# Where the last step of two layer norms runs: VectorE's subtract-and-multiply, or ScalarE's scale and bias per token

## The reference

```
def _layernorm(x, axis=-1, eps=1e-05):
    m = jnp.mean(x, axis=axis, keepdims=True)
    v = jnp.var(x, axis=axis, keepdims=True)
    return (x - m) / jnp.sqrt(v + eps)
...
x = _layernorm(x + _L0_attn_ref(x, W1, b1, Wp, bp))
x = _layernorm(x + _L0_ffn_ref(x, W_r, W_k, W_v, mu_r, mu_k))
```

## Time and profile before

| what | us |
|---|---|
| median of 3 runs | 761.15 |
| lowest and highest | 760.0, 762.69 |
| the profiled execution, its own time | 761.43 |
| its span in the profile | 759.7 |
| PE busy | 614.4 (81%) |
| DVE busy | 585.8 (77%) |
| ACT busy | 471.4 (62%) |
| POOL busy | 378.0 (50%) |

### The profile page before, as it was taken

How to read it: one execution, slowest core, us unless ns; L and a number is a source line. 1 busy time by engine, 2 the same in 40 slices (tenths; PEclk the granted TensorE clock), 3 DMA queues, 4 the chain that set the end, 5 groups by cost and what they waited for, 6 DMA issues and landing times.

```text
span 759.7 us, 17094 instructions
## 1 busy us (share of the span) xinstructions
PE 614.4 (81%) x6349; PEld 297.4 (39%) x6349; DVE 585.8 (77%) x1515; ACT 471.4 (62%) x918; POOL 378.0 (50%) x520
## 2 busy tenths in 40 slices
PE   2256888898888989898989888888989897987743
PEld 1013343444443535353434434443535353533232
DVE  3067888879889898979798989889898989792231
ACT  1110677686867676767777676767676776677510
POOL 6110334364555555565555464655655565455533
PEclk9999999999999999999999999999999999999755
DMA  2241213131322323131413131322323231100100
GB/s 55 92 101 44 91 54 115 44 113 45 98 73 60 112 58 115 51 121 36 120 33 118 41 128 45 79 93 58 113 58 115 45 109 33 47 17 16 29 14 14
DMA packets 63320, 53.29 MB, mean 70 GB/s; under 512 B 8706, under 2 KB 59012, under 8 KB 63236
## 3 DMA queue, kind: packets, MB, share of 16 engines
q1 hardware_dynamic: 63236, 52.20, 24.1%
HBM read 34.87 MB, written 17.30 MB: 69 GB/s over the span
## 4 chain that ended last, share of the span: by engine, by line
PE 50%; DVE 33%; ACT 6%; issue 5%; POOL 2%; DMA 2%; SPq 1%; POOLq 0%; DVEq 0%; ACTq 0%
DVE rowmax L632 16%; PE ops L481 12%; PE tps L433 8%; PE spare L372 8%; PE sps L450 8%; PE spare L386 5%; ACT probs L562 4%; DVE h L689 4%; DVE rowmax L636 3%; PE spare L412 2%; PE sps L457 2%; DVE result L689 2%; DVE attn L670 2%; DVE stats L643 2%; PE sps L462 2%
## 5 line engine op out<-in xcount | busy, mean ns | idle before, releaser
L562 ACT ACTIVATE probs<-tps 128x512 f32<-128x512 f32 x640 | 346.5, 595 | 139.4 <-PE tps L433 138.7
L632 DVE TENSOR_REDUCE rowmax<-sps 128x1 f32<-128x512 f32 (+2 forms) x768 | 342.5, 503 | 65.9 <-PE sps L462 62.2
L736 POOL TENSOR_SCALAR_AFFINE_SELECT probs<-probs 128x512 f32<-128x512 f32 x256 | 158.0, 635 | 262.6 <-ACT probs L562 262.6
L450 PE MATMUL sps<-kop,qop 48*128 48x128 bf16 (+3 forms) x1024 | 128.7, 310 | 62.5 <-DVE rowmax L632 35.7
L481 PE MATMUL ops<-probs,vop 128*32 128x384 f32 (+3 forms) x2048 | 172.7, 444 | 4.4 <-POOL probs L736 2.5
L433 PE MATMUL tps<-qop,kop 50*128 50x384 bf16 (+3 forms) x1024 | 126.4, 304 | 29.8 <-ACT probs L562 29.8
L636 DVE TENSOR_REDUCE rowmax<-sps 128x2 f32<-128x512 f32 x128 | 82.3, 685 | 15.6 <-PE sps L462 14.7
L433 PEld LDWEIGHTS tps<-qop,kop 50*128 50x128 bf16 x1024 | 34.5, 94 | 144.3 <-ACT probs L562 110.3
L450 PEld LDWEIGHTS sps<-kop,qop 48*128 48x128 bf16 x1024 | 40.5, 95 | 117.4 <-DVE rowmax L632 69.4
L457 PE MATMUL sps<-qmask,rows_of 64*128 64x256 bf16 (+1 forms) x640 | 83.7, 258 | 0.0
L481 PEld LDWEIGHTS ops<-probs,vop 128*32 128x32 f32 x2048 | 50.5, 109 | 77.4 <-issue 62.0
(11 more groups left out here) (73 smaller groups left out, 656.1 us busy)
## 6 DMA issues: line engine op xcount, KB each, us to landing
d_parts<-qk_parts SPq DMA_DIRECT2D x16, 768.0 KB, 3.5
qop<-d_parts SPq DMA_DIRECT2D x192, 32.0 KB
qop<-d_parts SPq DMA_DIRECT2D x64, 96.0 KB
kop<-d_parts SPq DMA_DIRECT2D x192, 32.0 KB
kop<-d_parts SPq DMA_DIRECT2D x64, 96.0 KB
xa<-L_attn_x SPq DMA_DIRECT2D x16, 256.0 KB, 3.0
xres<-L_attn_x SPq DMA_DIRECT2D x16, 256.0 KB, 3.4
out<-result SPq DMA_DIRECT2D x16, 256.0 KB, 2.5
```

The costliest lines, as they stand in the source:

```text
L450: nc.tensor.matmul(sps[:, bank(n + hh), off:off + w], qop[r, par, pair, BLK * a:BLK * a + BLK], kop[r, par, pair, 0:w], start=j == 0, stop ...
L562: nc.scalar.activation(probs[:, g % 2, i, :], tps[:, bank(4 * GROUPS * n + 4 * g + i), :], ACT.Exp, scale=SCALE)\
L632: last = nc.vector.reduce_max(rowmax[:, par, QUARTET * half + t, hh, a:a + 1], sps[:, bank(n), off:off + w], axis=AX_X)
L736: last = nc.gpsimd.affine_select(out=v, in_=v, compare_op=ALU.is_ge, fill=0.0, base=0, pattern=[[0, QUARTET], [1, BLK]], channel_multiplie ...
```

## The change

The form `(src - mean) * rstd`, one VectorE instruction for each 128 tokens, is replaced by `src * rstd + shift` on ScalarE, with `shift = -mean * rstd` formed on VectorE for the four blocks of 128 tokens in one instruction. `scale` and `bias` are given as one number per partition (token). The first norm keeps its place in group 7 but runs on ScalarE after the group's four exponentials; the second is in group 9 after its exponentials and ahead of `scale_steps`. VectorE's `shift` for the second norm is in group 8.

```
+            def normalise(i, n, src, dst, done_shift, done):
+                wait(act, done_shift, n + 1)
+                for t in range(TT):
+                    last = nc.scalar.activation(dst[:, t, :], src[:, t, :], ACT.Identity,
+                                                bias=shift[:, i, t:t + 1], scale=rstd[:, i, t:t + 1])
+                last.then_inc(done, 1)
...
+                    if g == 7 and active("D", b):
+                        wait(act, z_done, before("E", b))
+                        normalise(0, before("D", b), y, h[:, 1 - par], shift_done, h_done)
+                    if g == 9 and active("E", b):
+                        wait(act, stored, 16 * before("E", b))
+                        normalise(1, before("E", b), z, result, shift2_done, result_done)
                     if g == 9 and active("D", b):
                         scale_steps(before("D", b))
...
-            def normalise(i, n, src, dst, done_rstd, done):
+            def shift_of_mean(i, n, done_rstd, done_shift):
                 wait(dve, done_rstd, n + 1)
-                for t in range(TT):
-                    last = nc.vector.tensor_scalar(dst[:, t, :], src[:, t, :], moments[:, i, t, 0:1],
-                                                   rstd[:, i, t:t + 1], ALU.subtract, ALU.mult)
-                last.then_inc(done, 1)
+                nc.vector.scalar_tensor_tensor(shift[:, i, :], moments[:, i, :, 0], -1.0, rstd[:, i, :],
+                                               ALU.mult, ALU.mult).then_inc(done_shift, 1)
...
                     if g == 7 and active("D", b):
-                        wait(dve, z_done, before("E", b))
-                        normalise(0, before("D", b), y, h[:, 1 - par], rstd_done, h_done)
-                    if g == 9 and active("E", b):
-                        n = before("E", b)
-                        wait(dve, stored, 16 * n)
-                        normalise(1, n, z, result, rstd2_done, result_done)
+                        shift_of_mean(0, before("D", b), rstd_done, shift_done)
+                    if g == 8 and active("E", b):
+                        shift_of_mean(1, before("E", b), rstd2_done, shift2_done)
```

More of the change, by code:

```diff
@@ L180, in block_program @@
         rstd = sb("rstd", [P, 2, TT])
+        shift = sb("shift", [P, 2, TT])
         h = sb("h", [P, 2, TT, E])
@@ L235, in block_program @@
         rstd_done = sem("rstd_done")
+        shift_done = sem("shift_done")
         h_done = sem("h_done")
@@ L245, in block_program @@
         rstd2_done = sem("rstd2_done")
+        shift2_done = sem("shift2_done")
         result_done = sem("result_done")
```

## The result

| | us |
|---|---|
| changed kernel, median of 6 runs | 770.33 (767.13 to 774.01) |
| kernel before, beside it, 6 runs | 762.74 (760.0 to 764.36) |
| ratio, 95% interval | 1.0112 (1.0078 to 1.0146) |
| the profiled execution of the changed kernel | 767.13, span 765.4 |

The account below looks back on a forecast made before the run. TensorE and VectorE were the two busy engines (81% and 77%), with both norms on the chain. Terms summed to +3.75 us on the profiled 761.43, giving 765.2; 765.0 was predicted, range 757 to 774.

Parts of the forecast that it names:

- The price of the new instruction: On ScalarE: 495 ns for each 128x128 activation with two pointers, 0.385 us in a row, 1.54 us a norm.
- Rivals 1 and 2: ScalarE's small instructions: 1, cheap enough, not slower, 747 at the lower bound, chance 0.3; 2, no overlap, 778, chance 0.05.
- `shift`: On VectorE: 0.1 us for each, bounded by 0 and 0.16, with no wait to speak of.
- Group 8: In a full step, TensorE no longer waits 1.24 us for VectorE's maximum before `sps`; gain 0.74 us.
- Group 0: `result` ahead of `scaled` delays exponentials; TensorE waits some 1.6 us for ScalarE, leaving a full step at +0.02 us.
- The draining steps: End of b = 14 +0.8; b = 15 +0.1 and +0.95; b = 16 +0.7 and +0.4; last `result` +0.7 us.
- the sum: All terms over the whole kernel, full steps and those with fewer stages: 3.75 us slower, also given as 3.8.
- Rival 3: Group 8's gain is real and group 0 absorbs the delay: 0.1 to 0.2 us a step kept, 762 to 764; chance 0.15.
- Two of the signs named: Per full step: ScalarE busy +4.0 us, VectorE busy about -3.0; chain shares of both move by about 3 us each step.

Follow-up runs that it names:

- changed, again: The changed kernel, unedited, timed again on another occasion: 770.38 us, ratio 1.0106.
- changed, wait filled: Also called the filled kernel: the changed kernel plus 12 unused TensorE transposes in group 0 of b = 2 to 15; 766.50 us, ratio 1.0056.
- draining steps on VectorE: The changed kernel, but with `h` of b = 15 and 16 and `result` of b = 14 to 17 back on VectorE; 763.10 us, ratio 1.0028.
- `result` alone: The changed kernel with `h` back on VectorE, only `result` on ScalarE in group 9; 783.12 us, ratio 1.0262.
- one half: The changed kernel with `result` back on VectorE, only `h` on ScalarE; 752.77 us, ratio 0.9883.

## Why the prediction was right, and where its size was off

The profiles, cut at the start of `y` in b = 2 and in b = 14, say where the time went (us):

| profile | up to b = 2 | b = 2 to 14 | b = 14 to the end | span |
|---|---|---|---|---|
| before | 174.8 | 488.5 | 96.5 | 759.7 |
| changed | 173.7 | 488.8 | 102.9 | 765.4 |
| changed, again | 174.2 | 493.2 | 103.0 | 770.4 |
| changed, wait filled | 176.0 | 487.3 | 99.3 | 762.6 |

- **The price of the new instruction.** 495 ns alone and 1.54 us of ScalarE for a norm had been taken from the rows of other shapes; 487 ns and 1.54 us came out. Rivals 1 and 2, both about this price, fall with it. By the Trainium skill, "ScalarE: Activation LUTs", section "What ACT_TABLE_LOAD costs", the estimate is 479 ns, and 386 ns in a row; the trace agrees (487, and 1.54 / 4 = 385).
- **`shift`** took 155 ns, 0.05 more than taken, and nobody waited for it in a full step.
- **Group 8.** 0.74 us of gain forecast. TensorE's `osum` transposes start 5.18 us after group 7's exponentials (389.88 - 384.70), before 6.00 (391.92 - 385.92): 0.82.
- **Group 0.** The delay of the exponentials ate it up as forecast: the net of a full step is -0.10 us (+0.02 forecast), and from b = 2 to 14 the filled kernel, which has no fall there, needs 1.1 us less than the kernel before. The length of TensorE's wait was mis-stated as 1.6 us; it is 2.18. The prediction's own rows give it: the wait of 0.74 us ahead of `sps` goes away as well as the 0.74 of group 8, so TensorE comes to the place at 397.99 - 0.74 - 0.74 = 396.51, and the forecast start at 398.70 makes the wait 2.19. For the schedule this changes nothing, as ScalarE alone decides when the wait ends. For the clock it does.
- **The draining steps.** 3.6 us forecast (3.75 less the full steps and b = 1). From `y` of b = 14 to the end, the filled kernel needs 2.8 us more than the kernel before, but not at the same clock: in the kernel before, the clock fell at 704.6 us and for good at 714.8, in the filled one only at 719.3. The kernel with these norms back on VectorE held its clock there until 717.6. Against it the filled one needs 5.0 us more (99.25 and 94.24), where the same terms, with the 0.74 of group 8 that stays, had given 4.4. The changed kernel, with its falls, needs 6.4 more than before.
- **What failed is a term that is not in the sum: the clock.** It was priced at zero, with full steps taken as running at 1.00. The filled kernel is 3.9 us faster than the changed one by the medians, and what is left over the kernel before, 766.50 - 762.06 = 4.4, is near the 3.8 of the sum. So about half of the 8.3 us between the changed kernel and the kernel before goes with the idle time that the transposes fill. By the table it is lost in two places. In the full steps it is 1.5 us with one fall and 5.9 with three, one of them longer; from b = 14 on it is 3.6 and 3.7, and there the wait of 2.48 us is followed by a fall both times. The filled kernel's execution began some 2 us later, so these don't add up to the difference of the medians; nor is the nearness of 4.4 to 3.8 a proof of the sum, since the table has only 2.8 - 1.1 = 1.7 us of it in the stretches that the change touches, and 1.2 ahead of them.
- **Rival 3** had a full step keep 0.1 to 0.2 us of gain, and 0.10 is what it keeps. Its reason, that group 0 absorbs the delay, did not hold (the wait stands there whole), and its time, 762 to 764, would have come out without the clock's part and with the shorter end: 12 x -0.10 + 2.8 is 1.6 us more than before.
- **Two of the signs named were wrong.** ScalarE's busy time was to rise by 4.0 us a step; over 16 batches it is 2.85 each (45.6 / 16), while VectorE's falls by 2.66 for the 3.0 named. The 4.0 added up 8 x 495 ns, though the prediction itself has the instructions overlap. And the chain's shares were to move by about 3 us a step; VectorE's went from 33% to 11%, some 167 us in all, since maxima left the chain too (L632 had 16%, L648 has 6%) and exponentials took their place.

**When the clock fell.** Of the ten profiles four have the wait of 2.18 us in group 0 unfilled, 12 times each: the changed kernel (one fall), the same again (three), the one with the draining steps on VectorE (one), and `result` alone (five). All ten falls in full steps begin between 0.3 us before the end of such a wait and 1.5 us after it. The wait of 2.48 us at the head of b = 15, in three of the profiles, was followed by a fall within 1.6 us every time, with the clock down for 7 to 10 us. Waits of up to 1.25 us (0.72 to 0.86 in group 0, 1.1 to 1.24 behind VectorE, 0.96 to 1.17 at the head of b = 15) had none behind them, neither in a full step nor at the head of b = 15. How often 2.18 us brings a fall stays open, and so does what sets one such wait apart from the next in the same execution. Whether it is the one wait's length or TensorE's work around it wasn't separated.

## What to carry to other kernels

Moving work from a busy engine to one with a lower busy share pays only at a place where that engine idles: moving `result` cost 0.7 us a step in group 9, ahead of `scaled`, and gained 0.5 (40.05 to 39.52) in group 8, where ScalarE waited for TensorE. Split such a change into its moves and price each from the receiving engine's timeline; here one half was worth -9 us and the other +21. And read the receiving engine's delay twice: once for what it does to the schedule, and once for the one long wait of TensorE that it puts in place of three short ones. Before two executions are compared, look where they part: here up to 4 us of difference stood ahead of all that was edited.

## What the runs showed of the hardware

- TensorE's granted clock fell to its lower level, mostly for some 3.3 us, at a wait of 2.18 us between stretches of dense work, in 10 of 48 such waits; such a fall costs about 1.5 us (42.27 - 40.76; 43.14 - 41.57 = 1.57). After a wait of 2.48 us it fell in three of three. The kernel before, with waits of up to 1.24 us in a full step, had no fall there.
- Useless transposes in that wait made two kernels faster, by 3.9 us and 4.7 us.
- From 60 us into the span up to a time between 81 and 90 us TensorE ran mostly at the lower level (the projection took 2.07 us there, 1.13 after). The time of the rise differed between executions by 8 us, the start of `y` in b = 2 by 4.
- The subtract-and-multiply on VectorE had very different durations in the kernel before, by its groups of instructions:

```profile
L689 DVE TENSOR_SCALAR h<-y,moments,rstd 128x128 f32<-128x128 f32 x64 | 29.3, 519 | 0.8 <-POOL rstd L757 0.8
...
L689 DVE TENSOR_SCALAR result<-z,moments,rstd 128x128 f32<-128x128 f32 x64 | 23.0, 421 | 1.8 <-POOL rstd L757 1.8
```

Where the other engines were quiet, four took 1.11 us together, against the 1.86 us of `h` on the chain. Of the 128 instructions, 98 took 331 to 347 ns and 30 took 656 to 1179. Of the 30, 29 overlapped in time with GpSimd's mask (L736), by 0.62 to 0.71 us; of the 98, 83 did not overlap it at all, and the others by less than 0.2 us. That they go together is shown; a run with the mask moved away was not made. The same work on ScalarE took 477 to 494 ns each in the changed kernel, and up to 528 for `result` in group 8.
